# Splitting the aggregation of a quad around the next K turn and score product in a graph attention kernel

## The chip, the cores and the metric

The kernel runs on one core of a Trainium2 chip. A core has TensorE (PE, matrix products and transposes into PSUM), VectorE (DVE), ScalarE (ACT), GpSimd (POOL) and SyncE (SP), which run their own instruction streams and meet only through semaphores; DMA queues move data between HBM and the on-chip memory SBUF. The metric is the time of one execution in microseconds (us), lower is better; a number is a median of several runs.

## What is computed

The input is 3125 nodes of 512 features and 53,125 edges (25,000 in both directions and one loop per node), sorted by their target. The block is: layer norm, a graph attention of two layers, a linear attention ("mix") on the same normed input, and a mixture of eight experts. Only the graph attention bears on the change:

```python
for l in range(2):
    q = ((x @ Wq[l].T + bq[l]) * scaling).reshape(n, H, DH)      # H = 8 heads of DH = 64
    k = (x @ Wk[l].T).reshape(n, H, DH)
    v = (x @ Wv[l].T).reshape(n, H, DH)
    scores = einsum('ehd,ehd->eh', q[tgt], k[srcidx])            # one row per edge
    m = segment_max(scores, tgt)
    p = exp(scores - m[tgt])
    s = segment_sum(p, tgt)
    w = p / (s[tgt] + 1e-16)
    agg = segment_sum(w[:, :, None] * v[srcidx], tgt)
    x = x + agg.reshape(n, D) @ Wo[l].T + bo[l]                  # then norms and a small MLP
```

## The kernel before

**Tiles.** The edge stage of a layer works on 416 tiles of 128 edges. Four tiles are a quad (104 per layer, index g), two quads are a batch (j, 52 per layer); x is g modulo 2. For each tile POOL gathers 128 rows of K and V (4 KB each, 1024 numbers) from the table `KVd` in HBM into one of the buffers `kvs`: 14 of them in the first layer (layer 0 in the code), 17 in the second, in a ring. Once per batch it fetches the queries (L812) and scatters the sums (L818).

**One quad on TensorE** (`attend_pe`). A K turn is four transposes of the tile's K (L876, `turn_k(n)`) into one of two PSUM banks; ACT or DVE copies the bank to `kT` in SBUF (ACT L1055 for tiles 0, 2 and 3 of a quad, DVE L994 for tile 1). A score product (`score(n)`, L897 and L899) multiplies it with the queries into a bank of its own. DVE takes the minimum of a quad's scores (L987), ACT the exponentials with their sums (L1074), DVE divides (L998, L1001), TensorE turns the probabilities (L883, `turn_p`), DVE copies them out (L982, `empty_p`). The aggregation, `gather(g)`, then makes for each of 8 heads and 4 tiles one product of 32 columns of probabilities with 64 columns of V (L911): 32 products, which the trace records as 64 instructions. They sum into one bank, `AG`, for a whole batch; DVE copies it to `stage` (L1007). Once per batch come the turn of the one-hot tile (L857, with L859 in the first layer; even quads) or of the queries (L868; odd quads).

**Order.** It is written out by hand. In iteration g TensorE runs: K turn 0; K turn 1 and score 0; the whole `gather(g - 2)`; K turn 2 and score 1; K turn 3, score 2, the one-hot or query turn, score 3; `turn_p(g - 1)`. In the first layer a step of the mix attention (`next(side)`: L568, L593 and others) stands in each of the four places `next(side, None)`; in the second there is none.

**Waits around it.** The turns go to the two banks in strict alternation (`turn_table`), so each turn waits until the turn before the last was copied out: K turn 1 of a quad waits until the probabilities turned just before K turn 0 are copied (L982). A gather waits for that same copy. The last product of a gather raises the semaphore `agg`, and three engines wait for it: POOL in `fetch` (L803: with 14 or 17 buffers, tiles are fetched four at a time when a quad's buffers come free), DVE in `empty_p` two quads on, and DVE in `empty_agg` once per batch.

## Time and profile before

| | us |
|---|---|
| median of 3 runs | 3883.64 |
| lowest, highest | 3872.12, 3889.37 |
| the profiled execution | 3888.6 |
| its span on the core | 3887.3 |
| edge stage of the first layer in it, roughly | 345 to 1500 |
| edge stage of the second layer in it, roughly | 1980 to 3110 |

The profiled execution lies 5 us above the median. The edge stages are recognized in the trace by their gathers (L911); what lies before, between and after them are projections, norms, the mix attention's rest and the experts. Times in rows are counted from the start of the span. A row of the timeline is one or more instructions of one line on one engine; its bracket is the idle time of the engine ahead of it and what ended that. The releaser is inferred. The ends of TensorE's instructions are modelled in the trace; the start of the engine that waits for them is not.

### The profile page before, as it was taken

What the parts mean: (1) busy time and instruction counts of PE and PEld (TensorE: products, weight loads), DVE (VectorE), ACT (ScalarE), POOL (GpSimd) and SP (SyncE); (2) the same over time, 40 slices, a digit from 0 to 9 for tenths busy, and PEclk for the clock granted to TensorE, in tenths of its full rate; (3) what the DMA queues carried; (4) which work ended last, traced back from release to release, by engine and by line L of the source; (5) the groups of instructions that cost most, each with busy time, mean ns of one, the idle gap of its engine ahead of it and who ended that gap; (6) DMA issues with size and microseconds to landing.
All of it is one profiled execution on the core that took longest, in us unless ns stands there. A gap on an engine that the chain in (4) does not pass through costs nothing.

```text
span 3887.3 us, 76578 instructions
## 1 busy us (share of the span) xinstructions
PE 3170.7 (82%) x31682; PEld 2103.9 (54%) x31682; DVE 1581.0 (41%) x3186; ACT 1237.7 (32%) x3833; POOL 1095.8 (28%) x1109
## 2 busy tenths in 40 slices
PE   4997999999999996878967777777777768599899
PEld 3874666656666663437845555555555524244444
DVE  5113444444444444272123333333333334755654
ACT  3213445444444441111223333333333301122221
POOL 0003444444444440000034444444444300111200
PEclk7998999999999997989988888888888889789999
DMA  8225666666566552202256566656666522101100
GB/s 297 95 99 214 215 220 216 210 209 199 200 200 199 201 199 81 73 34 82 98 192 217 200 214 206 204 199 216 210 208 208 172 61 83 33 33 39 49 24 23
DMA packets 216466, 595.91 MB, mean 153 GB/s; under 512 B 36143, under 2 KB 42927, under 8 KB 216104
## 3 DMA queue, kind: packets, MB, share of 16 engines
q0 software_dynamic: 137088, 466.78, 36.0%
q1 hardware_dynamic: 79015, 124.04, 9.4%
q8 instruction: 259, 4.24, 0.5%
q14 instruction: 104, 0.84, 0.1%
HBM read 519.56 MB, written 96.89 MB: 159 GB/s over the span
## 4 chain that ended last, share of the span: by engine, by line
PE 32%; another core or an unknown queue 7%; issue 4%; DVE 4%; DMA 3%; POOL 3%; ACT 2%; SPq 0%; DVEq 0%; POOLq 0%; ACTq 0%
PE ps L876 4%; PE ps L2034 4%; PE ps L2055 4%; PE ps L911 3%; PE ps L899 2%; PE ps L1533 2%; DMA aggd<-stage,segs 2%; PE ps L443 2%; PE ps L445 2%; PE ps L444 2%; POOL Y L803 1%; DVE G L982 1%; PE ps L897 1%; PE ps L1470 1%
## 5 line engine op out<-in xcount | busy, mean ns | idle before, releaser
L803 POOL DMA_INDIRECT Y<-KVd,srcE x654 | 639.4, 978 | 1590.5 <-PE ps L911 725.2
L1055 ACT ACTIVATE work<-ps 128x512 f32<-128x512 f32 x624 | 367.0, 594 | 1088.8 <-PE ps L876 842.2
L876 PE MATMUL ps<-ident,Y 128*128 128x128 f32 x2616 | 454.3, 301 | 191.9 <-DVE G L982 134.2
L876 PEld LDWEIGHTS ps<-ident,Y 128*128 128x128 f32 x2616 | 329.9, 153 | 426.1 <-issue 221.0
L982 DVE COPY G<-ps 128x512 f32<-128x512 f32 x208 | 143.7, 691 | 579.6 <-remote 312.0
L568 PE MATMUL ps<-WA,xT 128*128 128x512 f32 (+1 forms) x600 | 329.5, 631 | 9.2 <-DMA G<-in_MpT 9.0
L897 PE MATMUL ps<-hotTs,maskA 128*128 128x128 f32 x832 | 276.6, 332 | 70.0 <-ACT work L1055 40.0
L1074 ACT ACTIVATE stage<-ps,stage 128x128 f32<-128x128 f32 x832 | 293.8, 369 | 84.3 <-DVE stage L987 83.9
L911 PE MATMUL ps<-Y,G 128*32 128x64 f32 x10464 | 276.5, 254 | 6.6 <-issue 3.5
L911 PEld LDWEIGHTS ps<-Y,G 128*32 128x32 f32 x10464 | 263.6, 134 | 10.2 <-DVE G L982 4.6
L443 PE MATMUL ps<-Wh,xs 128*128 128x512 f32 (+1 forms) x600 | 235.2, 392 | 18.9 <-DVE xs L394 18.9
L803 POOL DMA_INDIRECT G<-KVd,srcE x178 | 171.4, 963 | 239.5 <-PE ps L911 191.5
L444 PE MATMUL ps<-Wl,xs 128*128 128x512 f32 (+1 forms) x600 | 234.8, 391 | 0.0
L445 PE MATMUL ps<-Wh,xs 128*128 128x512 f32 (+1 forms) x600 | 234.6, 391 | 0.0
L897 PEld LDWEIGHTS ps<-hotTs,maskA 128*128 128x128 f32 x832 | 175.3, 211 | 106.7 <-issue 73.4
L994 DVE COPY work<-ps 128x512 f32<-128x512 f32 x208 | 143.9, 692 | 196.4 <-PE ps L876 188.9
L2055 PE MATMUL ps<-G,mt 128*128 128x512 f32 (+1 forms) x400 | 191.5, 611 | 33.0 <-DVE Y L2108 33.0
L2108 DVE SCALAR_TENSOR_TENSOR Y<-ps,WA,Y 128x512 f32<-128x512 f32 (+1 forms) x200 | 146.9, 748 | 152.5 <-PE ps L2055 143.1
L876 PE MATMUL ps<-ident,G 128*128 128x128 f32 x712 | 130.8, 313 | 83.2 <-DVE G L982 69.5
L2034 PE MATMUL ps<-xT,G 128*128 128x512 f32 (+1 forms) x448 | 198.5, 592 | 0.0
L899 PE MATMUL ps<-work,G 128*32 128x128 f32 x3328 | 192.7, 307 | 0.0
L899 PE MATMUL ps<-work,qblk 128*32 128x128 f32 x3328 | 190.4, 304 | 0.0
(279 smaller groups left out, 4920.6 us busy)
## 6 DMA issues: line engine op xcount, KB each, us to landing
KVd<-stage SPq DMA_DIRECT2D x96, 256.0 KB, 2.0
aggd<-work SPq DMA_DIRECT2D x2, 7936.0 KB, 26.7
Qd<-stage SPq DMA_DIRECT2D x48, 256.0 KB, 2.0
G<-aggd SPq DMA_DIRECT2D x48, 256.0 KB, 3.6
Y<-KVd,srcE POOLq DMA_INDIRECT x654
Y<-in_x SPq DMA_DIRECT2D x4, 1536.0 KB, 14.3
mixd<-mt SPq DMA_DIRECT2D x24, 256.0 KB
stage<-in_x SPq DMA_DIRECT2D x24, 256.0 KB, 3.3
```

Source lines behind the costliest of these rows:

```text
L443: pe.matmul(PS[e % 4][0:r, :], xh, Wh[:, w, k, :], start=(k == 0), stop=False)
L444: pe.matmul(PS[e % 4][0:r, :], xh, Wl[:, w, k, :], start=False, stop=False)
L445: mm = pe.matmul(PS[e % 4][0:r, :], xl, Wh[:, w, k, :], start=False, stop=(k == 3))
L568: mm = pe.matmul(bank[0:r, :], src, w[:, k, :], start=(k == 0), stop=(k == 3))
L803: pool.indirect_dma_start(out=kvs[a], out_offset=None, in_=KVd[l][:, :], in_offset=bass.IndirectOffsetOnAxis(ap=srcE[:, n:n + 1], axis=0)) ...
L876: mm = pe.transpose(bank[:, k * P:(k + 1) * P], kvs[a][:, k * P:(k + 1) * P], ident[:, :])
L897: pe.matmul(bank[:, at], maskA[:, c, :], hotT[j % 3], start=True, stop=False, skip_group_check=True)
L899: mm = pe.matmul(bank[32 * k:32 * k + 32, at], qblk[j % 2][:, k, 2 * (c % 4) + c // 4, :], kT[n % 3][:, k * P:(k + 1) * P], start=False, s ...
L911: mm = pe.matmul(AG[32 * i:32 * i + 32, DH * h:DH * (h + 1)], probs[x][:, i, h, :], kvs[a][:, D + DH * h:D + DH * (h + 1)], start=(x == 0 ...
L1055: act.activation(kT[n % 3], TB_[PLACE["k", n] % 2][:, :], ACT.Copy).then_inc(out_a, 1)
L2034: mm = pe.matmul(ups[u % 2][:, 0:cn], Wm1[:, k, x, :], xT[:, k, c0:c0 + cn], start=(k == 0), stop=(k == 3))
L2055: pe.matmul(down[d % 3][0:r, :], hid[(8 * c + x) % 4][:, o0:o0 + r], Wm2[:, x, :], start=True, stop=True).then_inc(dn_mm, 1)
```

## The change

`gather` gets a second argument: part 0 makes heads 0 to 3, part 1 heads 4 to 7. Part 0 stands where the whole gather stood and has its waits; part 1 stands after K turn 2 and score 1, and only its last product raises `agg`. The rest of the diff renames things or leaves them as they are: `banks(l)` is the same pair of banks, `len(kT)` is 3 in both layers, and `PACED` is 0, so its wait is never emitted.

```diff
-            def gather(g):
+            def gather(g, y):
                 x = g % 2
-                is_emptied(pe, l, PLACE["p", g])
-                if x == 0 and g:
-                    pe.wait_ge(ev, NJ * l + g // 2)
-                for h in range(H):
+                if y == 0:
+                    is_emptied(pe, l, PLACE["p", g])
+                    if x == 0 and g:
+                        pe.wait_ge(ev, NJ * l + g // 2)
+                for h in range(4 * y, 4 * y + 4):
                     for i in range(4):
...
-                mm.then_inc(agg, 1)
+                if y:
+                    mm.then_inc(agg, 1)
...
                 if g >= 2:
-                    gather(g - 2)
+                    gather(g - 2, 0)
                 next(side, None)
                 if g < NQ:
                     turn_k(4 * g + 2)
                     score(4 * g + 1)
+                if g >= 2:
+                    gather(g - 2, 1)
                 next(side, None)
```

TensorE in the second layer, one quad, from K turn 1 to score 2. Before (L876 K turn, L897 and L899 score, L911 gather):

```order
L876 MATMUL ps<-ident,Y 128x128 [waits kv_in0,out_d]
L876 MATMUL ps<-ident,Y 128x128 x3
L897 MATMUL ps<-hotTs,maskA 128x128 [waits out_a,exps]
L899 MATMUL ps<-work,qblk 32x128 x4
L911 MATMUL ps<-Y,G 32x64 [waits out_d]
L911 MATMUL ps<-Y,G 32x64 x31
L876 MATMUL ps<-ident,Y 128x128 [waits kv_in1,out_a]
L876 MATMUL ps<-ident,Y 128x128 x3
L897 MATMUL ps<-hotTs,maskA 128x128 [waits out_d]
L899 MATMUL ps<-work,qblk 32x128 x4
L876 MATMUL ps<-ident,Y 128x128 [waits kv_in2,out_d]
```

The same place now (L882 K turn, L903 and L905 score, L918 gather), from the first part of the gather on:

```order
L918 MATMUL ps<-Y,G 32x64 x15
L882 MATMUL ps<-ident,Y 128x128 [waits kv_in1,out_a]
L882 MATMUL ps<-ident,Y 128x128 x3
L903 MATMUL ps<-hotTs,maskA 128x128 [waits out_d]
L905 MATMUL ps<-work,qblk 32x128 x4
L918 MATMUL ps<-Y,G 32x64 x16
L882 MATMUL ps<-ident,Y 128x128 [waits kv_in2,out_d]
L882 MATMUL ps<-ident,Y 128x128 x3
L903 MATMUL ps<-hotTs,maskA 128x128 [waits out_a]
```

Sixteen of the 32 products moved behind one K turn and one score; the last of them, which raises `agg`, now stands right ahead of K turn 3.

TensorE in the first layer, the same place of a quad, where steps of the mix attention (L568; now L569) stand between. Before:

```order
L911 MATMUL ps<-Y,G 32x64 x31
L568 MATMUL ps<-WA,xT 128x512
L876 MATMUL ps<-ident,G 128x128 [waits kv_in12,out_a]
L876 MATMUL ps<-ident,G 128x128 x3
L897 MATMUL ps<-hotTs,maskA 128x128 [waits out_d]
L899 MATMUL ps<-work,G 32x128 x4
L568 MATMUL ps<-WA,xT 128x512
L876 MATMUL ps<-ident,G 128x128 [waits kv_in13,out_d]
```

And now:

```order
L918 MATMUL ps<-Y,G 32x64 x15
L569 MATMUL ps<-WA,xT 128x512
L882 MATMUL ps<-ident,G 128x128 [waits kv_in12,out_a]
L882 MATMUL ps<-ident,G 128x128 x3
L903 MATMUL ps<-hotTs,maskA 128x128 [waits out_d]
L905 MATMUL ps<-work,G 32x128 x4
L918 MATMUL ps<-Y,G 32x64 x16
L569 MATMUL ps<-WA,xT 128x512
L882 MATMUL ps<-ident,G 128x128 [waits kv_in13,out_d]
```

Here `agg` moved behind one mix step, one K turn and one score. The streams of the other engines hold the same instructions in the same order.

## Rows read from the trace of the kernel before

**Rows 1.** Page, part 2: TensorE clock granted, 40 slices of the span, tenths.

```profile
PEclk7998999999999997989988888888888889789999
```

**Rows 2.** Windows: stretch, length; busy us PE, PEld, DVE, ACT, POOL; clock, DMA share, GB/s.

```profile
430.00:830.00 400.00, 383.56 (x5318) 248.42 (x5316) 188.12 (x419) 194.20 (x761) 193.07 (x192) 1.00 0.65 215
...
2017.50:2041.80 24.30, 19.16 (x367) 14.48 (x368) 10.44 (x20) 10.96 (x35) 14.32 (x14) 1.00 0.77 249
...
2062.90:3100.00 1037.10, 750.04 (x11784) 580.09 (x11784) 329.35 (x621) 370.59 (x1154) 453.55 (x474) 0.82 0.62 206
```

**Rows 3.** Windows of L911 alone (PE, PEld), 64 records a gather, the same stretches.

```profile
430.00:830.00 400.00, 40.91 (x2432) 38.79 (x2432) 1.00 0.65 215
...
2017.50:2041.80 24.30, 4.09 (x192) 3.63 (x192) 1.00 0.77 249
2062.90:3100.00 1037.10, 172.88 (x6144) 166.32 (x6144) 0.82 0.62 206
```

**Rows 4.** Waits, 2062.9 to 3100 us: engine, line, releaser, total us, times, longest.

```profile
DVE G L982 <- remote: 307.6, 62, 6.7
ACT work L1055 <- remote: 216.6, 65, 5.2
...
PE ps L876 <- DVE G L982: 195.7, 82, 4.0
```

**Rows 5.** Timeline, second layer, a slow even quad: start us, length us, engine, line.

```profile
2096.22 1.12 PE L876 MATMUL ps<-ident,Y 128*128 128x128 f32 x4
...
2097.74 0.66 PE L876 MATMUL ps<-ident,Y 128*128 128x128 f32 x4
...
2099.70 0.66 PE L883 MATMUL ps<-ident,stage 128*128 128x128 f32 x4
...
2101.55 1.01 POOL L818 DMA_INDIRECT aggd<-stage,segs  x1 [0.31 <-issue]
2102.20 0.69 DVE L982 COPY G<-ps 128x512 f32<-128x512 f32 x1 [2.57 <-PE ps L876]
...
2102.95 0.66 PE L876 MATMUL ps<-ident,Y 128*128 128x128 f32 x4 [2.16 <-DVE G L982]
2103.62 0.60 ACT L1055 ACTIVATE work<-ps 128x512 f32<-128x512 f32 x1 [4.59 <-PE ps L876]
2103.68 0.69 DVE L994 COPY work<-ps 128x512 f32<-128x512 f32 x1 [0.19 <-PE ps L876]
```

**Rows 6.** Timeline, second layer near its start, a fast even quad.

```profile
2017.39 0.66 PE L876 MATMUL ps<-ident,Y 128*128 128x128 f32 x4
...
2018.40 0.66 PE L876 MATMUL ps<-ident,Y 128*128 128x128 f32 x4
...
2020.35 0.66 PE L883 MATMUL ps<-ident,stage 128*128 128x128 f32 x4
...
2022.00 0.69 DVE L982 COPY G<-ps 128x512 f32<-128x512 f32 x1 [1.85 <-PE ps L876]
...
2022.71 0.60 ACT L1055 ACTIVATE work<-ps 128x512 f32<-128x512 f32 x1 [3.03 <-PE ps L876]
```

**Rows 7.** Windows of 2 us in the slow quad of rows 5, columns as rows 2.

```profile
2100.30:2102.30 2.00, 0.49 (x5) 0.25 (x3) 0.10 (x1) 0.00 (x0) 1.69 (x2) 1.00 1.01 360
...
2104.30:2106.30 2.00, 1.93 (x53) 1.82 (x57) 0.69 (x3) 1.31 (x8) 0.00 (x0) 0.50 0.63 249
```

**Rows 8.** Timeline, first layer, an even quad; the gather ahead ends near 617.7 us.

```profile
622.38 0.66 PE L883 MATMUL ps<-ident,stage 128*128 128x128 f32 x4
...
625.17 0.69 DVE L982 COPY G<-ps 128x512 f32<-128x512 f32 x1 [2.27 <-PE ps L876]
...
625.34 0.60 ACT L1055 ACTIVATE work<-ps 128x512 f32<-128x512 f32 x1 [3.62 <-PE ps L876]
...
626.19 0.60 PE L876 MATMUL ps<-ident,Y 128*128 128x128 f32 x4
```

More of the change, by code:

```diff
@@ L28 @@
 ON_DVE = (1,)
+PACED = 0
 FAR = 8192.0
@@ L494, in edge_views @@
             onehot = [Y[:, 12288 + P * i:12288 + P * (i + 1)] for i in range(2)]
-            return kvs, probs, qblk, onehot
+            kT = [work[:, i, :] for i in range(3)]
+            return kvs, probs, qblk, onehot, kT
         def join_views(Y, G):
@@ L515, in crowd_views @@
                 take(HC, 2 * NJ).rearrange("p (j k) -> p j k", k=2) for _ in range(2)]
-        kvs, probs, qblk, onehot = edge_views(Y, G, 0)
-        TB_, SC, AG = [PS[3], PS[4]], [PS[5], PS[6]], PS[7]
+        kvs, probs, qblk, onehot, kT = edge_views(Y, G, 0)
+        TURN_BANKS, SC, AG = [[PS[3], PS[4]], [PS[3], PS[4]]], [PS[5], PS[6]], PS[7]
         smin = stage[:, 1, 0:ET]
@@ L521, in build @@
         qslot = stage[:, 3, :]
-        kT = [work[:, i, :] for i in range(3)]
         hotT = [hotTs[:, i, :] for i in range(3)]
@@ L782, in build, with banks @@
         PLACE, EMPTIED, TURNS, EMPTIES = turn_table()
+        def banks(l):
+            return TURN_BANKS[l]
         def kv_before(l, a):
@@ L802, in fetch @@
                     pool.wait_ge(agg, NQ * l + (n - KV) // 4 + 1)
+                    if PACED and n - PACED < ET and (n - KV) % 4:
+                        is_turned(pool, l, "k", n - PACED)
                 pool.indirect_dma_start(out=kvs[a], out_offset=None, in_=KVd[l][:, :],
@@ L849, in bank_of @@
                 e = PLACE[kind, n]
-                if e >= 2:
-                    is_emptied(pe, l, e - 2)
-                return TB_[e % 2]
+                if e >= len(banks(l)):
+                    is_emptied(pe, l, e - len(banks(l)))
+                return banks(l)[e % len(banks(l))]
             def turn_hot(j):
@@ L899, in score @@
                     mm = pe.matmul(bank[32 * k:32 * k + 32, at], qblk[j % 2][:, k, 2 * (c % 4) + c // 4, :],
-                                   kT[n % 3][:, k * P:(k + 1) * P], start=False, stop=True, skip_group_check=True)
+                                   kT[n % len(kT)][:, k * P:(k + 1) * P], start=False, stop=True, skip_group_check=True)
                 mm.then_inc(sc, 1)
-            def gather(g):
+            def gather(g, y):
                 x = g % 2
-                is_emptied(pe, l, PLACE["p", g])
-                if x == 0 and g:
-                    pe.wait_ge(ev, NJ * l + g // 2)
-                for h in range(H):
+                if y == 0:
[3 more added lines that the diff above has]
+                for h in range(4 * y, 4 * y + 4):
                     for i in range(4):
@@ L951, in bank_of @@
                 is_turned(dve, l, kind, n)
-                return TB_[PLACE[kind, n] % 2]
+                return banks(l)[PLACE[kind, n] % len(banks(l))]
             def one_hot(j):
@@ L991, in empty_k @@
                 bank = bank_of("k", n)
-                if n >= 3:
-                    dve.wait_ge(sc, ET * l + n - 2)
-                dve.tensor_copy(kT[n % 3], bank[:, :]).then_inc(out_d, 1)
+                if n >= len(kT):
+                    dve.wait_ge(sc, ET * l + n + 1 - len(kT))
+                dve.tensor_copy(kT[n % len(kT)], bank[:, :]).then_inc(out_d, 1)
             def normalise(g):
@@ L1052, in empty_k @@
                 is_turned(act, l, "k", n)
-                if n >= 3:
-                    act.wait_ge(sc, ET * l + n - 2)
-                act.activation(kT[n % 3], TB_[PLACE["k", n] % 2][:, :], ACT.Copy).then_inc(out_a, 1)
+                if n >= len(kT):
+                    act.wait_ge(sc, ET * l + n + 1 - len(kT))
+                act.activation(kT[n % len(kT)], banks(l)[PLACE["k", n] % len(banks(l))][:, :], ACT.Copy).then_inc(out_a, 1)
             def empty_q(j):
@@ L1060, in empty_q @@
                     act.wait_ge(sc, ET * l + NCH * (j - 1))
-                bank = TB_[PLACE["q", j] % 2]
+                bank = banks(l)[PLACE["q", j] % len(banks(l))]
                 for y in range(2):
@@ L1704, in build @@
         Yt = Y[:, :].rearrange("p (t d) -> p t d", t=NT)
-        kvs, probs, qblk, onehot = edge_views(Y, G, 1)
+        kvs, probs, qblk, onehot, kT = edge_views(Y, G, 1)
         part, wide, fixm, fixl, lastm, smin_l, ssum_l = join_views(Y, G)
```

## The prediction

> **What bounds the kernel now.** I read the page's clock line first. It shows full speed through the edge stage of the first layer and about 0.8 through that of the second [rows 1]. So I split the edge stages into windows. In the steady part of the first layer TensorE is busy 383.56 of 400 us (0.96) at a clock of 1.00; in the second it is busy 750.04 of 1037.1 us (0.72) at 0.82 [rows 2]. Counting gathers (L911, 64 records each) gives the length of a quad: 2432 / 64 = 38 quads in 400 us, 10.53 us each, in the first layer; 6144 / 64 = 96 quads in 1037.1 us, **10.80 us** each, in the second; but 192 / 64 = 3 quads in 24.3 us, **8.10 us** each, in a stretch near the second layer's start [rows 3]. The same instructions can thus run a quarter faster. The first layer is bound by TensorE; the second by a chain of waits.
>
> The list of waits names it: TensorE's K turn waits for L982, the copy of the turned probabilities, 82 times, 195.7 us in all (2.4 us each), and L982 itself waits 307.6 us for something that the trace calls remote [rows 4]. The timeline of a slow quad shows what that is. The gather ended near 2096.3, when K turn 2 (L876, 2096.22) follows it. The turn of the probabilities (L883) is recorded from 2099.70 to 2100.36, 4.1 us after the gather. L982 needs nothing later than that turn, and starts at 2102.20, 1.84 us late. The next quad's K turn 0 comes directly behind L883 and should end near 2100.8, yet ACT's copy of it (L1055) starts at 2103.62. TensorE stands still for 2.16 us [rows 5]. So TensorE's results are seen late, or its recorded ends are too early; either way its consumers start late. This happens while transfers are dense: TensorE is busy 0.49 of 2.00 us and the DMA share is 1.01; 4 us later TensorE works again, but at a clock of 0.50 [rows 7]. The half clock makes a gather 172.88 / 96 = 1.80 us long instead of 40.91 / 38 = 1.08 us [rows 3].
>
> In the fast quad the gather ends near 2017.5, the turn ends at 2021.01, 3.5 us after it, L982 starts at 2022.00 (4.5 us after, 1.0 late) and L1055 at 2022.71 (5.2 us after) [rows 6]. In the slow quad the same two starts are at 5.9 and 7.3 us [rows 5]. The transfers of a quad are released by `agg`, at the gather's end, so I measure everything from there.
>
> **The change part by part.** *The split itself.* No instruction is added: 64 records a gather stay. Two more changeovers between score and gather cost nothing that a row shows; 0.
>
> *What moves.* From `agg` to the turn of the probabilities there is one K turn and one score less; from the copy L982 to the next `agg` there is one more. That is 2018.40 - 2017.39 = 1.01 us at full clock [rows 6] and 2097.74 - 2096.22 = 1.52 us when part of it is at half clock [rows 5]. In the first layer a mix step moves with them: TensorE is busy 383.56 / 38 = 10.09 us a quad there and 19.16 / 3 = 6.39 us in the fast stretch without mix [rows 2, 3], so a step is about 3.7 / 4 = 0.9 us, and 1.9 us move. If nothing else reacted, the sum would be zero.
>
> *What reacts, second layer.* The probabilities' turn now ends 3.5 - 1.0 = 2.5 us after `agg` at full clock. Between the slow and the fast quad, 0.6 us earlier in the turn made L982 start 1.4 us earlier and L1055 2.1 us earlier. So the transfers' dense phase delays less what comes early in it. I bound L982's new start by 2.5 (no delay) and 5.9 us (the slow quad), and take 3.7, one microsecond late as in the fast quad, to which it is nearest. L1055 then starts near 4.5 us (bounds 3.0 and 7.3) and ends at 5.1 with its 0.60 us. Score 0 and half a gather (0.43 + 0.54, from 1.08 / 2) end near 6.1, K turn 2 near 6.7. Score 1 needs DVE's copy of K turn 1, L994, which started 2103.68 - 2096.3 = 7.4 us after the gather in the slow quad; bounds 5.2 and 7.4, so with its 0.69 us it ends between 5.9 and 8.1. Score 1 and the second half then take 1.0 us: 7.7 to 9.1 us, and 0.4 more if the clock still halves once per quad. I take **9.2 us** for a quad, near the upper end, since the clock is uncertain and the fast stretch had slightly fewer transfers (14 on POOL in 3 quads, 4.7 each, against 474 in 96, 4.9 each [rows 2]). Gain 10.80 - 9.2 = 1.6 us, x 104 quads = 166 us. Bounds: 10.80 - 7.7 = 3.1 us (-322), and a loss, which is the first rival.
>
> *What reacts, first layer.* There is 0.04 x 10.53 = 0.4 us of idle time per quad to win, at most 44 us. More can be lost. L982 starts at 625.17 and ends at 625.86, 8.2 us after the gather; K turn 1, which waits for it, starts at 626.19, so today it is covered by 0.33 us [rows 8]. K turn 1 moves from 8.5 to 8.5 - 1.9 = 6.6 us. If the copy keeps its place, TensorE waits 1.6 us; if it moves up with its turn, as above, nothing. I take 0.3 us, x 104 = +31 us; bounds -44 and +83 (1.6 us in the 52 even quads, which rows 8 shows).
>
> *Waits moved.* POOL's fetches (L803), with scatter and query fetch behind them on its queue, start 1.0 us (first layer 1.9 us) later in the quad. The list of waits holds no row in which TensorE's K turn waits for a transfer, so tiles land early; 0, and if that cover is gone up to 1 us a quad. DVE's copy of the sums (L1007) waits for `agg` once per batch and has L982 behind it, which starts at least 2.5 us after `agg`; 0. K turn 2 asks ACT for a copy half a gather earlier; ACT is busy 370.59 of 1037.1 us [rows 2] and the second half gather covers the copy; 0.
>
> **Sum.** 3888.6 - 166 + 31 = 3753.6 us for the profiled execution, which lay 5.0 us above the median: **3749 us**. With gains of 0.7 to 2.9 us a quad in the second layer and -20 to +80 us in the first this case spans 3640 to 3830.
>
> **The rivals.** *Slower: the late phase ends at a fixed time.* If what is held back comes free only when the burst of transfers that `agg` started is through, 7.3 us after `agg` whatever stands in it, then turning the probabilities earlier wins nothing, and the K turn and score moved behind L982 are added: 1.0 us at full clock, 1.5 at half. L1055 at 7.3 us in the slow quad [rows 5] and at 7.6 in the first layer [rows 8] speaks for it: quads of different work, nearly one time. The fast quad, 5.2 us, speaks against it [rows 6]. It decides where L982 starts later than 7.3 - 1.0 = 6.3 us after `agg`. Price: 104 x 1.0 = 104 us in the second layer and 52 x 0.9 = 47 (up to 83) in the first: 3883.6 + 151 = **4035 us**, to 4125 with half clock throughout.
>
> *No change: the delay belongs to the instructions.* If L982 follows its turn by 1.84 us wherever the turn stands, the microsecond won ahead of it is spent behind it, and the quads stay at 10.80 and 10.53 us: **3884 us**, within 15. Against it: the delay was 1.84 us in one quad and 0.99 in another [rows 5, 6]. The Trainium skill points this way: its page SBUF — State Buffer, section "Who interferes with whom", says that transfers have ports of their own and never contend with a compute engine. By that rule the transfers can't be what holds TensorE's results back, and the position inside the burst wouldn't matter. The rows show only that the two coincide, not that one causes the other.
>
> *Half a gain.* The chain shortens, but the clock still falls in each quad, so that the work behind L982 stays long: 0.7 us a quad, 3830 us; this is the end of the forecast's own range.
>
> **How the numbers follow.** The forecast 0.60, the fixed end 0.22, no change 0.13, and 0.05 for a small gain in the second layer that the first layer's loss eats. A measurement of this kernel can tell some 0.5% (19 us) from no change. Faster by more: the forecast's 0.60 and 0.01; within: 0.13 and 0.02; slower: 0.22 and 0.02, so 0.61, 0.15, 0.24. The range from 3630 to 4000 takes in the forecast, no change and the mild half of the losses; it leaves out most of the first rival and a little below, 2 in 10 together.
>
> **What would show it.** Right: in the second layer L982 starts 3 to 4.5 us after the last L918, quads of about 9 us, clock above 0.85, fewer and shorter waits of the K turn for the copy of the probabilities; in the first layer quads of 10.5 to 10.9 us. Wrong: L982 and ACT's copy at 5.9 to 7.3 us as before and quads of 11.8 us (first rival), or a start 1.8 us behind the turn and quads of 10.8 us (second). A wait of a K turn for a transfer would show that the later fetches matter.

## The result, and the profile after

| us | before | after |
|---|---|---|
| median (runs) | 3884.87 (8) | 3896.45 (8) |
| lowest, highest | 3867.93, 3891.55 | 3894.96, 3900.28 |
| profiled execution, its span | 3888.6, 3887.3 | 3899.3, 3898.0 |
| first layer, from the first `agg` to the last | 1147.0 | 1214.5 |
| second layer, the same | 1091.6 | 1030.3 |

The ratio is 1.0037, 95% interval 1.0024 to 1.0050: nothing that counts, and slower rather than faster. The first and last `agg` are taken at the end of the gather's last product. Behind the ratio stand a gain of 61.3 us in the second layer and a loss of 67.5 us in the first. In after, the K turn is L882, the turn of the probabilities L889, the score L903 and L905, the gather L918; DVE's copies are L992 (probabilities), L1004 (K turn 1) and L1017 (sums), ACT's copy of a K turn is L1065.

Windows of after, all engines (columns as in rows 2):

```profile
430.00:830.00 400.00, 375.57 (x5102) 245.83 (x5101) 180.54 (x401) 187.51 (x732) 180.86 (x184) 1.00 0.63 207
900.00:1380.00 480.00, 421.56 (x5331) 286.71 (x5333) 209.87 (x465) 206.19 (x769) 186.61 (x185) 1.00 0.55 184
2080.00:3100.00 1020.00, 804.18 (x12312) 608.31 (x12310) 340.60 (x652) 393.20 (x1214) 476.82 (x498) 0.84 0.66 219
```

The same stretches, L918 alone (PE, PEld), to be held against [rows 3]:

```profile
430.00:830.00 400.00, 47.42 (x2336) 43.03 (x2336) 1.00 0.63 207
900.00:1380.00 480.00, 52.51 (x2374) 45.85 (x2378) 1.00 0.55 184
2080.00:3100.00 1020.00, 218.47 (x6400) 177.26 (x6400) 0.84 0.66 219
```

At 64 records a gather, a quad now takes 1020 / 100 = 10.20 us in the second layer (10.80 before), 400 / 36.5 = 10.96 us in the first (10.53), and 480 / 37.1 = 12.9 us where the mix attention is in its second phase. Before, the same window of L911 held 2560 records, 40 quads of 12.0 us:

```profile
900.00:1380.00 480.00, 43.07 (x2560) 40.83 (x2560) 1.00 0.60 198
```

The waits of after, 2080 to 3100 us, against [rows 4]:

```profile
ACT work L1065 <- PE ps L882: 573.1, 295, 3.5
...
DVE stage L1017 <- DMA aggd<-stage,segs: 202.0, 49, 6.3
...
PEld ps L918 <- issue: 145.3, 198, 1.3
PE ps L918 <- issue: 120.9, 180, 1.2
...
DVE G L992 <- PE ps L882: 105.9, 59, 3.1
...
PE ps L882 <- DVE G L992: 62.1, 78, 1.7
```

The wait of the K turn for the copied probabilities fell from 195.7 to 62.1 us, as intended. In its place TensorE stands still inside the gather: 120.9 us in 180 pieces. Before the change that row was

```profile
PE ps L911 <- issue: 2.9, 4, 1.2
```

The timeline of after shows how. From here on "after `agg`" counts from the start of POOL's first fetch, which the traces show 0.3 us behind the end of the gather's last product; the prediction counts from that end. This is a quad of the second layer whose `agg` released POOL at 2302.36:

```profile
2302.36 0.96 POOL L809 DMA_INDIRECT G<-KVd,srcE  x1 [4.45 <-PE ps L918]
...
2305.36 0.66 PE L889 MATMUL ps<-ident,stage 128*128 128x128 f32 x4
2306.06 0.69 DVE L992 COPY G<-ps 128x512 f32<-128x512 f32 x1 [1.67 <-PE ps L889]
...
2306.82 0.60 ACT L1065 ACTIVATE work<-ps 128x512 f32<-128x512 f32 x1 [0.75 <-PE ps L882]
...
2307.56 0.30 PE L903 MATMUL ps<-hotTs,maskA 128*128 128x128 f32 x1
...
2309.46 0.69 DVE L1004 COPY work<-ps 128x512 f32<-128x512 f32 x1 [2.11 <-remote]
2309.79 0.66 PE L882 MATMUL ps<-ident,G 128*128 128x128 f32 x4
...
2310.20 0.33 PE L903 MATMUL ps<-hotTs,maskA 128*128 128x128 f32 x1
```

L992 starts 3.7 us and L1065 4.5 us after `agg`. Then score 0 (L903, 2307.56) and the first half of the gather go out, but K turn 2 starts only at 2309.79, 7.4 us after `agg`. The next quad (`agg` at 2311.64), PE alone, shows TensorE in that gap:

```profile
2316.34 0.52 PE L918 MATMUL ps<-Y,G 128*32 128x64 f32 x24
2317.30 0.24 PE L918 MATMUL ps<-Y,G 128*32 128x64 f32 x1 [0.44 <-issue]
2318.01 0.22 PE L918 MATMUL ps<-Y,G 128*32 128x64 f32 x1 [0.47 <-issue]
2318.73 0.42 PE L918 MATMUL ps<-Y,G 128*32 128x64 f32 x6 [0.51 <-issue]
2319.08 1.12 PE L882 MATMUL ps<-ident,Y 128*128 128x128 f32 x4
```

Single instructions of the gather start 0.71 us apart, and K turn 2 starts at 2319.08, again 7.4 us after `agg`, at a half clock: windows of after there give

```profile
2316.70:2318.60 1.90, 0.61 (x14) 0.14 (x2) 0.87 (x2) 0.55 (x4) 0.93 (x1) 1.00 0.95 328
2318.60:2321.50 2.90, 2.77 (x51) 2.48 (x51) 0.00 (x0) 0.60 (x1) 0.00 (x0) 0.54 0.59 217
```

These two quads are no exceptions: in the 49 quads whose gather ends between 2100 and 2600 us, K turn 2 starts 7.6 to 8.0 us after the gather's last product. So the late phase is still there and still ends near 7.4 us after `agg`. The change moved the probabilities out of it, and half a gather, K turn 2 and score 1 in or behind it.

The loss of the first layer comes from the same late phase. A quad of after whose `agg` came at 591.9:

```profile
591.91 0.96 POOL L809 DMA_INDIRECT Y<-KVd,srcE  x1 [3.97 <-PE ps L918]
...
596.16 0.69 DVE L992 COPY G<-ps 128x512 f32<-128x512 f32 x1 [1.54 <-PE ps L889]
596.33 0.60 PE L882 MATMUL ps<-ident,Y 128*128 128x128 f32 x4
...
599.09 0.60 ACT L1065 ACTIVATE work<-ps 128x512 f32<-128x512 f32 x1 [5.35 <-PE ps L882]
...
599.83 0.30 PE L903 MATMUL ps<-hotTs,maskA 128*128 128x128 f32 x1 [1.02 <-ACT work L1065]
```

K turn 0 is through at 596.93; ACT sees it at 599.09, 7.2 us after `agg`. Behind that stand score 0, half a gather, a mix step, K turn 2, score 1 and the other half, until 603.6: 11.7 us. Before the change K turn 1, score 0 and the gather stood between the end of the late phase and the next `agg`, a mix step and a score less [rows 8]. More of the loss lies later in the layer: 39 of the 67 us come in its second 52 quads, most of them in the second phase of the mix attention, from which no quad is shown here. Every second quad takes 15.1 us there; on a chip where nothing is late (below) the same kernel takes 13.0 us for it.

### The profile page after: what moved, and what is told of

Its sections match the earlier page's. It is cut to its first block, busy times and chain, and to the rows that moved or that the text cites. A ratio compares the mean times of both kernels' runs of the same rounds, so it can differ in the third digit from the quotient of the medians.

```text
span 3898.0 us, 76578 instructions
## 1 busy us (share of the span) xinstructions
PE 3218.5 (83%) x31682; PEld 2122.4 (54%) x31682; DVE 1579.9 (41%) x3186; ACT 1241.7 (32%) x3833; POOL 1089.8 (28%) x1109
## 4 chain that ended last, share of the span: by engine, by line
PE 40%; issue 5%; DVE 4%; ACT 2%; DMA 1%; POOL 0%; another core or an unknown queue 0%; SPq 0%; DVEq 0%; POOLq 0%; ACTq 0%
PE ps L882 7%; PE ps L918 5%; PE ps L2044 4%; PE ps L905 4%; PE ps L2065 4%; PE ps L1543 2%; PE ps L444 2%; PE ps L445 2%; PE ps L446 2%; DVE G L992 1%; PE ps L903 1%; PE ps L889 1%; PE ps L874 1%; PE ps L1480 1%; PE ps L2055 1%
## 5 line engine op out<-in xcount | busy, mean ns | idle before, releaser
L1065 ACT ACTIVATE work<-ps 128x512 f32<-128x512 f32 x624 | 368.5, 595 | 1131.3 <-PE ps L882 1113.9
L882 PE MATMUL ps<-ident,Y 128*128 128x128 f32 x2616 | 449.9, 299 | 63.8 <-DVE G L992 45.9
L882 PEld LDWEIGHTS ps<-ident,Y 128*128 128x128 f32 x2616 | 329.0, 152 | 286.6 <-issue 185.2
L918 PE MATMUL ps<-Y,G 128*32 128x64 f32 x10464 | 330.7, 238 | 101.3 <-issue 97.6
L569 PE MATMUL ps<-WA,xT 128*128 128x512 f32 (+1 forms) x600 | 331.9, 635 | 24.3 <-ACT G L752 14.7
L903 PE MATMUL ps<-hotTs,maskA 128*128 128x128 f32 x832 | 275.0, 331 | 89.0 <-ACT work L1065 71.0
L918 PEld LDWEIGHTS ps<-Y,G 128*32 128x32 f32 x10464 | 278.9, 122 | 119.5 <-issue 113.2
L992 DVE COPY G<-ps 128x512 f32<-128x512 f32 x208 | 143.9, 692 | 369.5 <-PE ps L889 195.7
L1004 DVE COPY work<-ps 128x512 f32<-128x512 f32 x208 | 143.9, 692 | 291.7 <-PE ps L882 204.2
L903 PEld LDWEIGHTS ps<-hotTs,maskA 128*128 128x128 f32 x832 | 174.8, 210 | 140.0 <-issue 75.6
L905 PE MATMUL ps<-work,G 128*32 128x128 f32 x3328 | 191.9, 306 | 0.0
L905 PE MATMUL ps<-work,qblk 128*32 128x128 f32 x3328 | 190.0, 303 | 0.7 <-issue 0.7
L1543 PE MATMUL ps<-G,WA 128*128 128x512 f32 (+1 forms) x448 | 177.1, 553 | 9.1 <-ACT G L1574 9.1
```

What stands on the lines that cost most here:

```text
L569: mm = pe.matmul(bank[0:r, :], src, w[:, k, :], start=(k == 0), stop=(k == 3))
L882: mm = pe.transpose(bank[:, k * P:(k + 1) * P], kvs[a][:, k * P:(k + 1) * P], ident[:, :])
L903: pe.matmul(bank[:, at], maskA[:, c, :], hotT[j % 3], start=True, stop=False, skip_group_check=True)
L905: mm = pe.matmul(bank[32 * k:32 * k + 32, at], qblk[j % 2][:, k, 2 * (c % 4) + c // 4, :], kT[n % len(kT)][:, k * P:(k + 1) * P], start=Fa ...
L918: mm = pe.matmul(AG[32 * i:32 * i + 32, DH * h:DH * (h + 1)], probs[x][:, i, h, :], kvs[a][:, D + DH * h:D + DH * (h + 1)], start=(x == 0 ...
L1065: act.activation(kT[n % len(kT)], banks(l)[PLACE["k", n] % len(banks(l))][:, :], ACT.Copy).then_inc(out_a, 1)
```

## The experiments

Eighteen runs were made, in five series, each on one chip beside the kernel before. The chips turned out to be of two sorts, which I call late and prompt (the expectations call a late chip slow). Each chip was used for one series only, so whether the sort is the chip's own or its state at that time isn't shown. The kernel before took 3972, 3968 and 3959 us on three late ones (series 1, 3, 5), 3547 and 3549 us on two prompt ones (series 2, 4); the chip of the result, at 3884, is nearer to the late ones. On a prompt chip the semaphores that TensorE raises in the first layer of the unchanged code are seen within 0.05 us of its products' ends. On the late ones DVE's copy of the probabilities starts 2.2 us behind its turn there (even quads, 430 to 830 us), and 2.1 us on the chip of the result. Kernels with fetches left out use the rows of old tiles; the direct fetches and the half rows bring other rows. The last two columns give the time from the first to the last `agg` of a layer in the profiled run.

| series | kernel | median us | ratio (95%) | layer 1 | layer 2 |
|---|---|---|---|---|---|
| 1 late | split in the second layer only | 3851.8 | 0.969 (0.967, 0.971) | 1159.0 | 1039.8 |
| 1 | split in the first layer only | 4089.1 | 1.028 (1.026, 1.031) | 1272.2 | 1163.0 |
| 1 | whole, no later fetches | 3441.0 | 0.866 (0.863, 0.868) | 1112.5 | 677.0 |
| 1 | split, no later fetches | 3459.3 | 0.870 (0.868, 0.873) | 1121.8 | 673.9 |
| 2 prompt | whole, direct fetches in layer 2 | 3439.3 | 0.970 (0.968, 0.972) | 1117.9 | 680.5 |
| 2 | whole, half rows in layer 2 | 3452.3 | 0.974 (0.971, 0.976) | 1118.2 | 690.5 |
| 2 | whole, spaced fetches in layer 2 | 3661.1 | 1.032 (1.030, 1.035) | 1117.8 | 895.1 |
| 2 | split in layer 2 only, spaced there | 3658.8 | 1.032 (1.030, 1.034) | 1118.0 | 896.1 |
| 3 late | split in the second layer only | 3856.2 | 0.972 (0.970, 0.974) | 1155.3 | 1036.5 |
| 3 | split in the first layer only | 4079.5 | 1.028 (1.025, 1.031) | 1262.9 | 1161.1 |
| 3 | whole, direct fetches in layer 2 | 3490.5 | 0.879 (0.877, 0.882) | 1157.6 | 681.7 |
| 3 | whole, half rows in layer 2 | 3952.7 | 0.997 (0.995, 0.999) | 1158.2 | 1140.8 |
| 4 prompt | whole, three fetches a quad in layer 2 | 3449.6 | 0.972 (0.968, 0.976) | 1117.7 | 687.2 |
| 4 | split in layer 2 only, early scatter | 3443.0 | 0.970 (0.967, 0.973) | 1117.6 | 682.5 |
| 4 | the same, spaced fetches | 3443.2 | 0.970 (0.967, 0.973) | 1118.1 | 677.1 |
| 4 | the changed kernel itself | 3652.2 | 1.028 (1.024, 1.031) | 1126.5 | 875.4 |
| 5 late | split in layer 2 only, early scatter | 3847.0 | 0.971 (0.969, 0.974) | 1156.5 | 1041.8 |
| 5 | whole, early scatter; layer 1 three fetches | 3879.3 | 0.980 (0.977, 0.982) | 1121.1 | 1099.0 |

**One layer at a time** (series 1 and 3). `SPLIT` is (0, 1) or (1, 0) by layer:

```diff
                 if g >= 2:
                     gather(g - 2, 0)
+                if g >= 2 and not SPLIT[l]:
+                    gather(g - 2, 1)
                 next(side, None)
...
-                if g >= 2:
+                if g >= 2 and SPLIT[l]:
                     gather(g - 2, 1)
```

> The gather is split in the second layer only; in the first layer it is whole, as before the change. From the two traces: first to last gather took 1147.0 us before and 1214.5 after in the first layer (67.5 lost), 1091.6 and 1030.3 in the second (61.3 won). My theory, that the two layers act each for itself: about 3884 - 61 = 3823 us, ratio 0.984 to the kernel before. Rival, that the second layer's gain is drift between two profiled executions or hangs on what the first layer leaves: 3884, ratio 1.00.

> The gather is split in the first layer only. Theory, layers act each for itself: 3884 + 67 = 3951 us, ratio 1.017, with the loss in the second phase of the mix attention (every second quad 15.5 us long, 12.0 before). Rival, that the first layer's loss comes from elsewhere: 3884, ratio 1.00.

Signs as expected, sizes 2.0 and 1.7 times as large. Each run has one layer whole, which serves to judge the split layer of the other: 1163.0 - 1039.8 = 123 us won in the second layer, 1272.2 - 1159.0 = 113 us lost in the first. Series 3, on another late chip, gave 125 and 108:

> The gather split in the second layer only, once more: the kernel before took 3972 us on the chip of the first experiments and 3547 on that of the second, where TensorE's results were seen within 0.05 us in the untouched first layer. Theory A, the lateness is a state of the chip and the split acts only through it: if the kernel before takes 3850 us or more here, the ratio is 0.97 to 0.985; if it takes about 3550, the ratio is 0.995 to 1.01. Rival: the ratio is the same on every chip, 0.97.

> The gather split in the first layer only, once more. Theory A: if the kernel before takes 3850 us or more here, the ratio is 1.017 to 1.03; if about 3550, it is 1.00 to 1.007 (the order alone was worth 9 us without fetches). Rival: 1.028 on every chip.

The layers act each for itself; on late chips gain and loss nearly cancel, as in the result. What they are worth differs from chip to chip.

**No fetches** (series 1). The later tiles are not fetched:

```diff
                 while at < ET and (at - KV) // 4 <= g - 2:
-                    fetch(at)
                     at += 1
...
-                pe.wait_ge(kv_in[a], 16 * (kv_before(l, a) + n // KVN[l] + 1))
+                if n < KVN[l]:
+                    pe.wait_ge(kv_in[a], 16 * (l * (a < KVN[0]) + 1))
```

> The gather is whole in both layers, and the fetches of K and V after the first 14 (first layer) and 17 (second layer) tiles of 128 edges are left out: the ring's old tiles are used again, so POOL issues only the query fetch and the scatter, one or two transfers a batch, and the sums are of the wrong rows. Theory A, the transfers that agg starts hold back when TensorE's results are seen: the late phase shrinks, quads of the second layer fall from 10.8 to 7.0 to 7.7 us (TensorE is busy 6.4 us in one), about 3.3 x 104 = 340 us; the first layer wins 0.2 us a quad without and about 0.8 with the second phase of the mix, some 50 us: about 3500 us. Rival B, the delays belong to the instructions and their waits, or to the clock alone: quads of 10 us or more in the second layer, above 3800 us.

> As the run with the whole gather and without these fetches, but with the gather split in both layers. Theory A: both the gain of the second layer and the loss of the first come through the late phase; without it the split is worth within 0.2 us a quad either way: within 25 us of the whole gather without fetches. Rival B, the order of TensorE's instructions is worth 0.6 us a quad by itself: 60 us less in the second layer and 65 us more in the first, seen per layer in the trace.

Windows of the kernel with the whole gather, second layer, all engines:

```profile
2100.00:2600.00 500.00, 465.13 (x9300) 355.51 (x9297) 257.96 (x494) 290.55 (x912) 77.46 (x76) 1.00 0.08 24
```

TensorE is busy 0.93 of the time at full clock, and quads take 677 / 103 = 6.6 us: better than the 7.0 to 7.7 I expected. With the split, the second layer is 3 us shorter and the first 9 us longer. So of 113 us lost in the first layer some 9 belong to the order itself, and of 123 won in the second 3; all the rest comes through the fetches. Rival B, in which the delays or the order of the instructions do it alone, is refuted. The clock is at 1.00 here without any other change.

**Direct fetches and half rows** (series 2 and 3). What in the fetches does it? In the first kernel SP issues them as plain transfers (each with a semaphore of its own kind, left out here), in the second they bring 2 KB in place of 4 KB a row:

```diff
+        for n in range(KVN[1], ET):
+            if (n - KVN[1]) % 4 == 0:
+                sp.wait_ge(agg, NQ + (n - KVN[1]) // 4 + 1)
+            a = n % KVN[1]
+            r = P * (n % 24)
+            sp.dma_start(kvs[a], KVd[1][r:r + P, :]).then_inc(kv_hw[n % 13], 16)
```

```diff
-                pool.indirect_dma_start(out=kvs[a], out_offset=None, in_=KVd[l][:, :],
+                half = l == 1 and n >= KV
+                pool.indirect_dma_start(out=kvs[a][:, 0:D] if half else kvs[a], out_offset=None,
+                                        in_=Qd[1][:, :] if half else KVd[l][:, :],
```

> Gather whole in both layers. In the second layer the fetches after the first 17 tiles are issued by SP as plain transfers of 128 contiguous rows of 4 KB (the same 512 KB each, the same release by agg) in place of POOL's indirect ones; the rows are not the right ones. The first layer is untouched. Theory A1, POOL's issuing of indirect transfers (1 us each, four or five behind one agg) is what delays the sight of TensorE's results: quads of the second layer fall from 10.8 or more to 6.6 to 8 us, near the 6.6 us without these fetches: at least 300 us less. Theory A2, the bytes under way delay it (2 MB in 7.4 us are 283 GB/s): quads stay within 1 us of before.

> Gather whole in both layers. In the second layer the fetches after the first 17 tiles bring rows of 2 KB (from the table of q) instead of 4 KB, with the same number of POOL's indirect transfers and of rows: half the bytes, wrong rows. Theory A1, POOL's issuing: the late phase still ends 7.4 us after agg, quads stay within 0.5 us of before. Theory A2, the bytes: it ends near 4 us, quads of about 8 us, 250 us less.

Series 2 fell on a prompt chip and told nothing of the late phase. Both kernels won some 100 us there all the same; what the early scatter shows below fits that. The kernel before took 3547 us there. Its second layer has no trace on a prompt chip; it is worked out at about 788 us (7.7 us a quad) from series 4, where it took 3549.0 us and the kernel at 3443.0, with 682.5 us in that layer, differs from it there alone. On a late chip:

> The second layer's later fetches as plain transfers from SP, the same bytes, once more; the rows are not the right ones. On the chip of the first time nothing was late, so it told nothing of the late phase. If this chip is a slow one (the kernel before at 3850 us or more): theory A1, POOL's issuing makes the lateness: quads of 6.6 to 8 us in the second layer, 300 us or more below before; theory A2, the bytes under way make it: quads within 1 us of before, above 3800 us.

> The second layer's later fetches with rows of 2 KB from the table of q, as many indirect transfers with half the bytes, once more. If this chip is a slow one: theory A1, the number of POOL's indirect transfers counts: late phase to 7.4 us after agg and quads as before; theory A2, bytes count: late phase to about 4 us, quads of about 8 us, 250 us below before.

Windows, second layer, of the direct fetches on the late chip:

```profile
2100.00:2600.00 500.00, 464.31 (x9278) 355.06 (x9278) 256.55 (x491) 290.53 (x910) 77.64 (x76) 1.00 0.94 340
```

and of the half rows on the same chip:

```profile
2100.00:3000.00 900.00, 629.42 (x9800) 489.87 (x9800) 274.94 (x520) 309.26 (x960) 383.77 (x401) 0.80 0.38 107
```

All the bytes, at 340 GB/s and 0.94 of the transfer engines' time, leave TensorE alone; 107 GB/s issued by POOL's indirect transfers keep it at 0.70 busy, and ACT's copy of K turn 0 starts 7.5 to 7.6 us after the gather's last product, as with whole rows. So it isn't the bytes, and theory A2 falls; half of them are worth 20 of 480 us. Nor is it the number of packets: the direct fetches move 49480 in the 500 us, the kernel before 30147 (on the chip of the result). Theory A1 holds for POOL's indirect transfers as a whole. The direct fetches changed the issuing engine and the kind of transfer (contiguous rows in place of indexed ones) at once, and no run separates the two. This also bears on the page of my second rival. The Trainium skill's rule (SBUF — State Buffer, "Who interferes with whom"), that transfers don't contend with a compute engine, agrees with the direct fetches. It doesn't cover what goes with POOL's indirect ones, which cost (1161.1 - 681.7) / 103 = 4.7 us a quad on this chip. By what path they hold TensorE's results back, no run here shows.

**How long is the late phase?** Behind each `agg` POOL has five transfers, four fetches and a scatter or a query fetch, about 1.25 us apart. In the first quad shown above they are, behind the one at 2302.36:

```profile
2303.62 0.94 POOL L809 DMA_INDIRECT Y<-KVd,srcE  x1 [0.30 <-issue]
2304.87 0.94 POOL L809 DMA_INDIRECT Y<-KVd,srcE  x1 [0.30 <-issue]
2306.11 0.94 POOL L809 DMA_INDIRECT Y<-KVd,srcE  x1 [0.30 <-PE ps L889]
2307.35 1.03 POOL L818 DMA_INDIRECT stage<-Qd,segs  x1 [0.30 <-issue]
```

Two kernels issue four (the one of series 5 in the first layer, with `if l or` there):

```diff
                 while at < ET and (at - KV) // 4 <= g - 2:
-                    fetch(at)
+                    if l == 0 or (at - KV) % 4 != 3:
+                        fetch(at)
                     at += 1
```

> Gather whole in both layers; in the second layer every fourth fetch of the later tiles is left out (its old tile is used), so a quad has four of POOL's transfers behind agg and not five. Theory, the late phase is as long as the burst, 1.24 us for each transfer: it ends at 6.2 us after agg and not 7.4, and quads are 1.2 us shorter, about 125 us less than before (on a chip without lateness within 30 us). Rival, its length is fixed by something else: end at 7.4 us, no gain.

That one met a prompt chip, where it was expected to change nothing and won 99 us (see the early scatter). In the second series-5 kernel (below, with its expectation) the first layer had four transfers. Timeline of its first layer, an even quad, first fetch and copy of the probabilities (L1002 there):

```profile
597.20 0.95 POOL L810 DMA_INDIRECT G<-KVd,srcE  x1 [3.35 <-PE ps L926]
...
603.06 0.69 DVE L1002 COPY G<-ps 128x512 f32<-128x512 f32 x1 [0.91 <-PE ps L897]
```

and of the other kernel of that series, with five on the same chip (L1000 there):

```profile
599.18 0.95 POOL L810 DMA_INDIRECT G<-KVd,srcE  x1 [2.99 <-PE ps L924]
...
606.44 0.69 DVE L1000 COPY G<-ps 128x512 f32<-128x512 f32 x1 [0.89 <-PE ps L888]
```

The copy starts 5.9 us after the first fetch in place of 7.3: 1.4 us less for one transfer less. It is still held back. In the 19 or 20 even quads from 430 to 830 us the turn ends 5.4 to 5.5 us after the gather's last product in all these runs. The copy starts 7.5 to 7.6 us after it on a late chip with five transfers, 6.1 to 6.6 with four, and 5.4 to 5.6 on a prompt chip. The first layer took 1121.1 us in place of 1156.5, nearly the 1118 of a prompt chip. So here, in one run on a late chip, the late phase grew with the burst.

**Spaced fetches** (series 2). The second to fourth fetch of a quad also wait for a K turn (`PACED` is (0, 7) by layer):

```diff
                     pool.wait_ge(agg, NQ * l + (n - KV) // 4 + 1)
+                    if PACED[l] and n - PACED[l] < ET and (n - KV) % 4:
+                        is_turned(pool, l, "k", n - PACED[l])
```

> Gather whole in both layers. In the second layer the second, third and fourth fetch of a quad wait also for the K turn seven tiles ahead of them, so that they leave POOL one after another over the quad instead of in one burst behind agg. Theory A, a burst holds results back and gaps let them through: quads of about 9.5 us, 100 to 130 us less than before. Rival, spacing only spreads the lateness over the whole quad: ratio 1.00 or above.

> Gather split in the second layer only, with the same spacing of that layer's fetches. Theory A: a gain over the split in the second layer alone (0.969 on its chip, 61 us in the traces of the other): quads of 9.2 us, about 80 us less than that, 140 to 200 us below before. Rival: spacing brings nothing or costs, 0.97 to 0.985 of before.

On a prompt chip both cost 3.2%, as the rival of the first had it, for a reason I hadn't thought of. The waits of the whole, spaced kernel, 2100 to 2850 us:

```profile
DVE stage L1020 <- DMA aggd<-stage,segs: 225.1, 42, 7.4
PEld ps L883 <- DVE G L995: 169.8, 85, 5.5
```

The scatter of a batch stands behind the fourth fetch on POOL's queue. DVE's copy of the next sums may overwrite `stage` only when the scatter has landed, and the copy of the probabilities is queued behind it.

**The changed kernel on a prompt chip, and the early scatter** (series 4 and 5). The scatter is issued behind the quad's first fetch, in the second layer:

```diff
+                if l and g % 2 == 0 and 0 <= b - 2 < NJ:
+                    if at < ET:
+                        fetch(at)
+                        at += 1
+                    scatter(b - 2)
                 while at < ET and (at - KV) // 4 <= g - 2:
                     fetch(at)
                     at += 1
-                if g % 2 == 0 and 0 <= b - 2 < NJ:
+                if l == 0 and g % 2 == 0 and 0 <= b - 2 < NJ:
                     scatter(b - 2)
```

> The changed kernel itself, on the chip of these runs. Theory, the layers act each for itself: on a slow chip (before at 3850 us or more) loss and gain cancel, ratio 0.995 to 1.005; on a chip without lateness the orders alone differ, 1.00 to 1.007. Rival, the two splits hinder each other: 1.01 or more.

> Gather split in the second layer only, and there the scatter of a batch is issued behind the first fetch of the quad, not behind the fourth. The burst has the same five transfers. Theory: the late phase stays, DVE's wait for the scatter (122.7 us in 35 waits in the split second layer) was mostly a wait for agg itself: within 15 us of the split in the second layer alone, 0.970 of before on a slow chip. Rival, the scatter's landing held the next quad's copies: 30 to 60 us less than that.

> As the run with the early scatter, and the second to fourth fetch of a quad wait for the K turn seven tiles ahead of them. Theory A, one spaced transfer holds results back for about its own 1.24 us and the gaps let them through: quads of 9.3 us, about 90 us less than the split with the early scatter, ratio near 0.945 on a slow chip. Rival, every K turn releases a transfer that then holds back that turn's own copy, so that the chain of each tile is late: quads of 10 us or more, nothing won.

The changed kernel loses 2.8% there: 9 us in the first layer, as without fetches, and 875.4 - 788 = 87 us in the second. The rival number, 1.01 or more, was met. Its reason, that the two splits hinder each other, isn't what the trace shows, though the split of the second layer alone with the late scatter was not run on a prompt chip. The waits of the changed kernel on this chip, 2100 to 2800 us:

```profile
DVE stage L1017 <- DMA aggd<-stage,segs: 211.0, 41, 6.7
PEld ps L882 <- DVE G L992: 153.7, 80, 4.8
```

and its timeline:

```profile
2201.95 1.01 POOL L824 DMA_INDIRECT aggd<-stage,segs  x1 [0.30 <-issue]
...
2207.59 0.69 DVE L1017 COPY stage<-ps 128x512 f32<-128x512 f32 x1 [4.59 <-DMA aggd<-stage,segs]
2208.20 0.68 DVE L992 COPY G<-ps 128x512 f32<-128x512 f32 x1
...
2208.93 0.66 PE L882 MATMUL ps<-ident,Y 128*128 128x128 f32 x4 [2.44 <-DVE G L992]
```

The scatter leaves POOL at 2201.95, the sums' copy waits for its landing until 2207.59, the probabilities' copy stands behind that, and TensorE waits 2.44 us. With the early scatter the same wait (L1025 there, 2100 to 2600 us) is

```profile
DVE stage L1025 <- DMA aggd<-stage,segs: 25.4, 28, 2.4
```

and the second layer runs at 682.5 us, near the 677 without any fetch. (The windows hold about 41 and 38 batches.) That is 193 us less than the changed kernel, more than the 87 us that it had lost: the worked-out 788 us of the kernel before have some 100 us above that pace too. With the whole gather and the late scatter, the half rows, the direct fetches and the three fetches reached 690.5, 680.5 and 687.2 us on prompt chips, as if less ahead of the scatter did there what issuing it early does. How much of its 788 us the kernel before waits for the scatter was not traced. Spacing adds nothing that can be measured (0.970 both), where I had expected a gain on a late chip. The windows of the kernel with the early scatter:

```profile
2100.00:2600.00 500.00, 462.46 (x9194) 361.23 (x9193) 258.82 (x490) 288.04 (x901) 363.66 (x377) 1.00 0.95 340
```

POOL's indirect transfers bring 340 GB/s here, and TensorE is as busy as without them. What they do to TensorE on a late chip they don't do on this one. On a late chip:

> Gather split in the second layer only, the scatter there issued behind the quad's first fetch, once more. If this chip is a slow one (before at 3850 us or more): theory, the late phase is the bound and the scatter matters little, ratio 0.960 to 0.972 (0.9692 and 0.9716 with the late scatter); rival, the scatter's landing is a part of the loss there too, 0.94 or less. If before takes about 3550: 0.970 again.

> Gather whole in both layers; in the second layer the scatter is issued behind the quad's first fetch. In the first layer every fourth of the later fetches is left out (old tiles are used), which leaves four and not five of POOL's transfers behind agg there. Theory for the second layer: on a slow chip the whole gather stays late, 1163 us from first to last gather as before, and the split is what wins; on a chip without lateness the scatter alone gives the gain, 680 to 690 us (682.5 with the split). Rival: the scatter does nothing without the split. For the first layer on a slow chip, theory: what is seen late is seen at 6.2 us after agg and no longer at 7.4; rival: still at 7.4.

With the split, the early scatter brings nothing on a late chip (0.971 against 0.969 and 0.972). With the whole gather it brings some 45 to 60 us: the second layer took 1099.0 us in the profiled execution, where 1161 and 1163 were measured on other late chips, and that execution was 14 us below the median. I hadn't expected this. The traces (2100 to 2600 us) show where it comes from. In even quads, whose burst holds the scatter, the copy of the probabilities starts 6.1 us after the gather's last product (median) in place of 7.5; in odd quads, and for ACT's copy of K turn 0, it stays at 7.5. So the late phase is as long as before and lets one result through earlier. With the split that copy starts at 3.1 us in even quads either way, so there is nothing left to win.

The kernel with the split in the second layer alone and the early scatter is faster than the kernel before on both sorts of chip: 0.971 on a late one, 0.970 on a prompt one. Whether a prompt chip needs the split for it was not tried (without fetches the order of the second layer was worth 3 us), nor spacing with the early scatter on a late chip.

## Why the prediction was wrong, step by step

- **The bound of the second layer** was read rightly: a chain of waits, fed by results that are seen late while transfers run. The missing fetches and the direct ones show the link, and that it is to POOL's indirect transfers.
- **The split itself at 0** holds to 3 us in the second layer; in the first it costs 9 us of 1112.5.
- **L982 (now L992) at 3.7 us after the gather, ACT's copy at 4.5 us:** 4.0 and 4.8 us by the prediction's count in the first quad shown. Over the quads from 2100 to 2600 us the medians are 3.1 and 3.8 us in even quads, 3.8 and 4.6 in odd ones. This step was right.
- **"Score 0 and half a gather end near 6.1, K turn 2 near 6.7": this step failed.** By the prediction's count K turn 2 starts at 7.7 us in both quads shown and ends at 8.4 and 8.9; it should have ended at 6.7. I treated the late phase as a delay on the handing over of results. It also stops TensorE's own products (0.71 us from one to the next) and it ends no earlier for what has already escaped from it: in 49 quads K turn 2 starts 7.6 to 8.0 us after the gather. DVE's copy of K turn 1, at 7.4 us in the first quad and 4.5 us in the second, was at my upper bound once and below the lower one once. Behind the phase the clock was 0.54 in the second quad, as I had feared for the upper end. The quad is 10.20 us and not 9.2: 1.0 x 104 = 104 us.
- **The first rival** had the mechanism: an end at a fixed 7.3 us. It was given 0.22 with a wrong test ("it decides where L982 starts later than 6.3 us"). L982 did start early, and the fixed end caught the next thing. Its price was wrong too, since it kept the copy of the probabilities, and all that waits for it, at the end of the late phase and added the moved work behind that. The fast quad that I held against it had four of POOL's transfers and not five; the run with four in the first layer shows that this shortens the phase.
- **The second rival, no change,** named 3884 within 15 us, and 3896 was measured. That is luck. Its reason, that L982 follows its turn by a fixed 1.84 us, doesn't hold: from 2100 to 2600 us the median lateness behind the turn fell from 2.4 (even quads) and 3.0 us (odd) to 0.5 and 0.9. A gain of 61 us and a loss of 67 happened to cancel.
- **The first layer at +31 us** measured +67.5. I followed one chain, the copy of the probabilities to K turn 1, and asked only whether it would move up. It did (4.5 us after the gather). The next chain, K turn 0 to ACT's copy to score 0, was held to 7.5 us instead, and ahead of the next `agg` there is now more work. The row for it stood in [rows 8]: L1055 at 625.34, 7.6 us after the gather. The upper bound of 83 us held here, but not on the late chips of the series (113 and 108 us).
- **POOL's later fetches at 0, DVE's wait for `agg` at 0.** No K turn waits for a tile, right. But "scatter and query fetch behind them on its queue" was named and not followed to who waits for the scatter. With the split it costs nothing on late chips beside the late phase (0.971 with the early scatter, 0.969 and 0.972 without). On a prompt chip it is nearly the whole loss, 87 us.
- **The sum:** 3749 predicted, 3896 measured, inside the range of 3630 to 4000, which had been drawn to take in no change. The span of the forecast's own case was added up wrongly: gains of 0.7 to 2.9 us a quad and -20 to +80 us in the first layer give some 3560 to 3890 us, not 3640 to 3830, and so nearly reach the measurement. Of the difference of 147 us, 104 are the second layer's quad and 36 the first layer's.

## What to carry to other kernels

When a stall has a fixed end that something else sets, moving one victim out of it only chooses the next: list everything that will stand before that end after the change, the stopped engine's own instructions too, and count what is left to do behind it. Follow each queue that a release starts down to its last entry and to who waits for that; on a prompt chip the scatter at the end of POOL's queue was worth more than the reordering. And look for the cause rather than the symptom: four of POOL's indirect transfers in place of five shortened the late phase by 1.4 us, and the same bytes as direct transfers ended it. Both work with other rows than the result needs; a kernel with the right rows and without the late phase was not tried.

## What the runs showed of the hardware

- On a late chip POOL's indirect transfers hold back TensorE, and not by their bytes: with half the bytes the second layer took 1140.8 us against 1161.1, with the same bytes as direct transfers from SP 681.7. In the gap shown above TensorE starts one instruction in 0.71 us. On a prompt chip POOL brings 340 GB/s and TensorE is busy 462.46 of 500 us.
- Chips differ in this: the same kernel took 3547 and 3549 us on two, 3884 on one, 3959 to 3972 on three. The change is worth 1.004 on one chip and 1.028 on another, for different reasons.
- A scatter issued behind four fetches held DVE's copy until 5.6 us after its issue on a prompt chip. The waits for it came to 211.0 us in 700 us; issued behind the first fetch, to 25.4 us in 500 us.
- TensorE's clock, 0.82 on average in the second layer before, is 1.00 there once the stops are gone (465.13 of 500 us busy).
